# A two-layer mixture-of-experts block around a linear recurrence: value and gate projections formed during the inversion, silu by ScalarE alone, output projection ahead of the forget gate's products, roots by logarithm

## The reference, cut to what matters

```
x = x + 0.5 * ffn(layernorm(x))          # top 2 of 8 experts, x is [4, 1024, 256] float32
x = x + attn(layernorm(x))
x = x + 0.5 * ffn(layernorm(x))

attn:  q, k, v = silu(x@Wq), silu(x@Wk), silu(x@Wv)
       log_f = log_sigmoid(x @ Wf1 @ Wf2);  beta = 2*sigmoid(x @ Wbeta);  k = l2norm(k)
       recurrence over 1024 steps of a 32x32 state per head (decay, a rank-one correction, k v^T)
       y = out * sigmoid(x @ Wog1 @ Wog2);  y = y / sqrt(mean(y*y) + eps) * norm_w;  return y @ Wo
layernorm: (x - mean) / sqrt(var + eps)
```

## Time and profile before

| | |
|---|---|
| median of 3 runs (lowest, highest) | 2212.82 us (2205.81, 2214.22) |
| the profiled execution, its own time | 2211.96 us |
| its span, first to last instruction | 2210.2 us |
| mean granted TensorE clock | 0.846 of full speed |
| busy: PE, DVE, POOL, ACT | 1602.6 (73%), 1189.6 (54%), 735.4 (33%), 632.5 (29%) us |
| first layer of experts with its routing | 0 to 574 us |
| attention: begin; three looped passes; last pass | 574 to 638; 638 to 1490; 1494 to 1756 us |
| second layer of experts | 1758 to 2210 us |

### The profile page before, as it was taken

How to read it: one execution, slowest core, us unless ns; L and a number is a source line. 1 busy time by engine, 2 the same in 40 slices (tenths; PEclk the granted TensorE clock), 3 DMA queues, 4 the chain that set the end, 5 groups by cost and what they waited for, 6 DMA issues and landing times. The chain is left out here.

```text
span 2210.2 us, 62919 instructions
## 1 busy us (share of the span) xinstructions
PE 1602.6 (73%) x23284; PEld 1062.9 (48%) x23285; DVE 1189.6 (54%) x3478; ACT 632.5 (29%) x1646; POOL 735.4 (33%) x988
## 2 busy tenths in 40 slices
PE   4359999999477278572777536786357299999995
PEld 4336666666135265251643436444355156666663
DVE  7513434444256875559764696667766334344442
ACT  2111111111356234453343633446323111111110
POOL 3722222222044151550514704238044212222221
PEclk9999999999677587775887856886668599999998
DMA  9443223232101000110001000010000272323234
GB/s 293 146 160 48 45 45 45 46 45 39 52 3 28 1 19 20 41 30 0 20 20 40 10 20 15 5 58 9 3 11 29 95 233 45 48 43 48 43 48 100
DMA packets 83844, 113.32 MB, mean 51 GB/s; under 512 B 13048, under 2 KB 74944, under 8 KB 81600
## 3 DMA queue, kind: packets, MB, share of 16 engines
q1 hardware_dynamic: 57120, 75.91, 11.2%
q0 software_dynamic: 26592, 35.67, 9.7%
HBM read 63.65 MB, written 52.08 MB: 52 GB/s over the span
## 5 line engine op out<-in xcount | busy, mean ns | idle before, releaser
L591 PE MATMUL ffn_bank<-ffn_w,ffn_tileT 128*128 x1136 | 539.0, 597 | 7.4 <-DMA ffn_w<-in_w2t_dram 3.9
L712 POOL DMA_INDIRECT x<-ffn_yout,ffn_place x142 | 221.1, 1557 | 651.2 <-DVE ffn_yout L679 587.1
L650 ACT ACTIVATE ffn_gate<-ffn_bank 128x512 f32<-128x512 f32 x142 | 84.8, 597 | 706.2 <-PE ffn_bank L591 706.2
L607 PE MATMUL ffn_bank<-ffn_w,ffn_actT 128*128 x1136 | 268.6, 379 | 1.8 <-DVE ffn_actT L693 1.8
L591 PEld LDWEIGHTS ffn_bank<-ffn_w,ffn_tileT 128*128 128x128 f32 x1136 | 195.5, 192 | 148.7 <-issue 148.5
L607 PEld LDWEIGHTS ffn_bank<-ffn_w,ffn_actT 128*128 128x128 f32 x1136 | 215.7, 190 | 91.2 <-issue 69.2
L693 DVE COPY ffn_actT<-ffn_bank 128x512 f32<-128x512 f32 x142 | 98.1, 691 | 170.8 <-PE ffn_bank L599 170.8
L685 DVE TENSOR_TENSOR ffn_gate<-ffn_gate,ffn_bank 128x512 f32<-128x512 f32 x142 | 97.6, 687 | 167.1 <-PE ffn_bank L591 167.1
L1444 PE MATMUL at_bank<-pass_right,pass_left 32*32 32x48 f32 x3072 | 52.2, 231 | 83.0 <-DVE pass_right L1316 63.5
L580 PE MATMUL ffn_bank<-ffn_ident,ffn_tile 128*128 128x128 f32 x284 | 55.6, 278 | 77.5 <-DMA ffn_tile<-xs 77.3
L599 PEld LDWEIGHTS ffn_bank<-ffn_ident,ffn_gate 128*128 128x128 f32 x568 | 71.2, 141 | 73.9 <-issue 73.7
(11 more groups left out here) (493 smaller groups left out, 3252.1 us busy)
## 6 DMA issues: line engine op xcount, KB each, us to landing
ffn_tile<-xs SPq DMA_DIRECT2D x142, 130.0 KB, 2.1
ffn_w<-in_w1t_dram SPq DMA_DIRECT2D x16, 1024.0 KB, 5.2
ffn_w<-in_w2t_dram SPq DMA_DIRECT2D x16, 512.0 KB, 6.2
ffn_x<-in_x_dram SPq DMA_DIRECT2D x16, 256.0 KB, 4.8
x<-ffn_x SPq DMA_DIRECT2D x16, 256.0 KB, 6.1
pass_xa<-x SPq DMA_DIRECT2D x12, 256.0 KB, 3.6
pass_xr<-x SPq DMA_DIRECT2D x12, 256.0 KB, 2.7
x<-pass_xr SPq DMA_DIRECT2D x12, 256.0 KB, 2.1
```

Source lines behind the costliest of these rows:

```text
L591: t = pe.matmul(bank[:, :], rowsT[b][:, k * P:(k + 1) * P], w1[:, bass.ds(e * 2048 + (k * 1024 + half * INNER), INNER)], start=(k == 0), s ...
L607: t = pe.matmul(p_y[b], actT[b][:, k * P:(k + 1) * P], w2[:, bass.ds(e * 1024 + k * DIM, DIM)], start=(k == 0), stop=(k == ICH - 1))
L650: act.activation(gate[b][:, :], p_g[b][:, :], ACT.Silu).then_inc(s_silu, 1)
L712: pool.indirect_dma_start(total, bass.IndirectOffsetOnAxis(ap=place[b][:, 0:1], axis=0), yout[b][:, :], None, compute_op=ALU.add).then_inc ...
```

## The change

- Value and gate projections leave `between`. They are formed in `invert`, on TensorE between the groups n = 7 and n = 8 that go back, and on ScalarE ahead of the third `compact`. `xT` and `fg` therefore last: `fg` has a buffer of its own, `xT` lies in the buffer of the gate `gt`, so its first copy waits until o times gate is done.
- silu is one ScalarE activation; VectorE's second step, the halved weights and the tanh buffers go. The k and q jobs (8 instead of 16) use banks 0 to 2 and no longer wait for `log_f`. The sums of squares of k stand in banks 3, 2, 0, 1, so the products with beta no longer wait for their reading; the first of them waits for the slot numbers.
- In `between` the output projection stands ahead of `fg` and the forget gate's products on TensorE; `fg` is copied by ScalarE; `log_f` stands on VectorE inside `choose_vector`, ahead of the wait for the counts.
- 1/sqrt(var) is Exp(-0.5 Ln(var)) on ScalarE with one Newton step of three dependent VectorE instructions (`refine`) in place of Sqrt and a reciprocal, in all layer norms. The Ln/Exp set is loaded ahead of use.

```diff
+def refine(dve, link, root, var, tmp):
+    link(dve.tensor_tensor(tmp[:, :], root[:, :], root[:, :], ALU.mult))
+    link(dve.scalar_tensor_tensor(out=tmp[:, :], in0=tmp[:, :], scalar=-0.5, in1=var[:, :], op0=ALU.mult, op1=ALU.mult))
+    link(dve.scalar_tensor_tensor(out=root[:, :], in0=tmp[:, :], scalar=1.5, in1=root[:, :], op0=ALU.add, op1=ALU.mult))
...
-        r.link(dve, dve.reciprocal(r.rstd[:, :], r.rstd[:, :]))
+        refine(dve, lambda ins: r.link(dve, ins), r.rstd, r.var, r.dm)
...
-        act.activation(self.rstd[:, :], self.var[:, :], ACT.Sqrt).then_inc(self.s_std, 1)
+        act.activation(self.rstd[:, :], self.var[:, :], ACT.Ln).then_inc(self.s_ln, 1)
+        act.wait_ge(self.s_ln, g + 1)
+        act.activation(self.rstd[:, :], self.rstd[:, :], ACT.Exp, scale=-0.5).then_inc(self.s_std, 1)
...
+        fg = last("fg", [FG, BATCH * PT])
+        xT = gt[:, :, :].rearrange("p (k c) t -> p k (c t)", k=KCH)
...
-                for t in (wq, wk, wv):
-                    dve.tensor_scalar(t[:, :, :], t[:, :, :], 0.5, None, ALU.mult)
...
# between
+    JOBS = [(t, w, g, c) for t, w in ((k, wk), (q, wq)) for g, c in QUARTERS]
+    SQUARES = [psum[i] for i in (3, 2, 0, 1)]
-            r = routing(..., sem, [psum[i] for i in (0, 1, 2, 2, 3, 0)])
+            r = routing(..., sem, [psum[0], psum[1]] + [psum[3][:, i * P:(i + 1) * P] for i in range(4)])
# between, TensorE
+                    if j >= 3:
+                        pe.wait_ge(s_ev, j - 2)
+                    for kc in range(KCH):
+                        i = pe.matmul(psum[j % 3][:, :], w[:, kc, g * P:(g + 1) * P], xT[:, kc, c * 512:(c + 1) * 512], ...)
...
                 if ends:
                     pe.wait_ge(s_yn, 4)
                     (output projection, 8 tiles)
                 if begins:
+                    pe.wait_ge(s_xt, NT)
+                    (fg in two halves into psum[0], psum[1])
+                    pe.wait_ge(s_fgc, 2)
+                    (the forget gate's four products into psum[4 + j])
                 if ends:
                     r.gate_tensor(pe, 0)
                 if begins:
-                    for j in range(2, EARLY + 4):
+                    for j in range(4):
                         job(j)
                 if ends:
                     r.count_tensor(pe, 0)
                 if begins:
-                    for j in range(EARLY + 4, len(JOBS)):
+                    for j in range(4, 8):
                         job(j)
                     for j in range(4):
                         pe.wait_ge(s_sq, j + 1)
-                        pe.wait_ge(s_gt, j + 1)
+                        pe.wait_ge(s_ev, min(j + 5, 8))
+                        if j == 0 and ends:
+                            pe.wait_ge(r.s_rows, 1)
# between, ScalarE, after the copies to xT: the new order
+                    act.copy(fg[:, 0:512], psum[0][0:FG, :])
                     r.std_scalar(act, 0)
+                    act.copy(fg[:, 512:1024], psum[1][0:FG, :])
                     (Abs of the four forget products)
                     r.turn_scalar(act, 0)
                     (Exp of the four)
                     r.choose_scalar(act, 0)
                     (Ln of the four)
+                    act.preload_act_table_set("silu_and_others")
                     (silu of jobs 0 to 3; tanh of beta's rows; silu of jobs 4 to 7)
                     act.preload_act_table_set("natural_log_exp_and_others")
# between, VectorE
+                    r.logits_vector(dve, 0)
+                    r.choose_vector(dve, 0, (lambda: [log_f(j) for j in range(4)]) if begins else None)
# invert, TensorE
                 if n == 8:
+                    for j, (t, g, c) in enumerate(VALUES):
+                        if j < 4:
+                            pe.wait_ge(s_bke, j + 1)
+                            for kc in range(KCH):
+                                t = pe.matmul(psum[j][:, :], wv[:, kc, g * P:(g + 1) * P], xT[:, kc, c * 512:(c + 1) * 512], ...)
+                        else:
+                            pe.wait_ge(s_vale, j - 3)
+                            t = pe.matmul(psum[j % 4][:, :], wrank[RANK:2 * RANK, g * P:(g + 1) * P], fg[RANK:2 * RANK, c * 512:(c + 1) * 512], ...)
+                        t.then_inc(s_val, 1)
+                    pe.wait_ge(s_vale, len(VALUES))
                     pe.wait_ge(s_tc, 3)
# invert, ScalarE
                 if n == 8:
+                    act.preload_act_table_set("silu_and_others")
+                    for j, (t, g, c) in enumerate(VALUES):
+                        act.wait_ge(s_val, j + 1)
+                        (j < 4: Silu of psum[j] to v; else Tanh of psum[j % 4], scale 0.5, to gt)
                     act.wait_ge(s_inv, STEPS - LAST // 2 + CT)
                     compact(slice(CT, CT + CT // 2), slice(0, CT))
```

More of the change, by code:

```diff
@@ L126, in __init__ @@
         self.p_t, self.p_g, self.p_c = banks[0:2], banks[2:4], banks[4:6]
-        (self.s_stat, self.s_var, self.s_std, self.s_xn, self.s_tr, self.s_xt, self.s_gate, self.s_sub, self.s_exp,
+        (self.s_stat, self.s_var, self.s_ln, self.s_std, self.s_xn, self.s_tr, self.s_xt, self.s_gate, self.s_sub, self.s_exp,
          self.s_both, self.s_cnt, self.s_rows, self.s_own) = (
-            sem("r_" + n) for n in "stat var std xn tr xt gate sub exp both cnt rows own".split())
+            sem("r_" + n) for n in "stat var ln std xn tr xt gate sub exp both cnt rows own".split())
         k = 64
@@ L910, in between @@
         if ends:
-            r = routing(lambda n, sh, dt=F32: sb("r_" + n, sh, dt, at=scope), sem, [psum[i] for i in (0, 1, 2, 2, 3, 0)])
+            r = routing(lambda n, sh, dt=F32: sb("r_" + n, sh, dt, at=scope), sem, [psum[0], psum[1]] + [psum[3][:, i * P:(i + 1) * P] for i in range(4)])
             if not begins:
@@ L1054, in _ @@
                     if begins:
+                        if ends and j == 0:
+                            act.wait_ge(s_y, 4)
                         turn(2 * j)
@@ L1061, in _ @@
                 if begins:
-                    if not ends:
-                        act.preload_act_table_set("natural_log_exp_and_others")
+                    act.wait_ge(s_fg, 1)
+                    act.copy(fg[:, 0:512], psum[0][0:FG, :]).then_inc(s_fgc, 1)
+                if ends:
+                    r.std_scalar(act, 0)
+                if begins:
+                    act.wait_ge(s_fg, 2)
+                    act.copy(fg[:, 512:1024], psum[1][0:FG, :]).then_inc(s_fgc, 1)
                     for j in range(4):
@@ L1067, in _ @@
                         act.activation(lg[j][:, :], psum[4 + j][:, :], ACT.Abs).then_inc(s_a, 1)
+                if ends:
+                    r.turn_scalar(act, 0)
+                if begins:
                     for j in range(4):
@@ L1070, in _ @@
                         act.activation(lg[j][:, :], lg[j][:, :], ACT.Exp, scale=-1.0).then_inc(s_e, 1)
+                if ends:
+                    r.choose_scalar(act, 0)
+                if begins:
                     for j in range(4):
@@ L1171, in _ @@
                 if begins:
-                    for j in range(EARLY):
-                        silu(j)
-                if ends:
-                    r.logits_vector(dve, 0)
-                    r.choose_vector(dve, 0, (lambda: [silu(j) for j in range(EARLY, EARLY + 4)]) if begins else None)
-                if begins:
-                    for j in range(EARLY + 4 if ends else EARLY, NKQV):
-                        silu(j)
                     dve.wait_ge(s_bt, 1)
@@ L1495, in invert @@
 def invert(nc, scope, sb, sem, psum, s, env, a_sb, a_top, tk, s_tk, regroup, z, nxt):
-    ident, ta, mask = (env[n] for n in ("ident", "ta", "mask"))
+    ident, ta, mask, xT, fg, wv, wrank, v, gt = (env[n] for n in "ident ta mask xT fg wv wrank v gt".split())
     def tb(name, shape):
```

127 lines of the change are left out of this document (45 added, 82 removed).

## The result

| | before | after |
|---|---|---|
| median of 5 runs, us | 2212.82 (2205.81 to 2214.22) | 2195.89 (2193.78 to 2198.17) |
| profiled execution: span / own time, us | 2210.2 / 2211.96 | 2196.3 / 2198.17 |
| granted clock | 0.846 | 0.847 |

The ratio is 0.9929, interval 0.9905 to 0.9954: faster by 17 us, where I had forecast 36. 2195.9 lies above my range, which ended at 2194.

A forecast was written before the change was run, and what follows sets the result against it. Attention blocks were taken as bound by order and waits, looped passes ending with the scatter chain behind the slot numbers. Passes -17.6, `begin` -19.5, costs +1.6: -35.5 against 2211.96 gives 2176.5 us; range 2166 to 2194.

The forecast's parts named there:

- Value and gate in the inversion, cost 0: All four inversions: added projections fit ScalarE's 26.54 us idle before the third `compact`, ending over 5 us early; cost 0.
- Rival E: Inversion: the projections overflow it, by ScalarE's writes or a late start; 3 us x 4 = +12, 2188; chance 0.06.
- rival F: silu: Tanh not in its table set, two loads more in each place; `begin` 0 to 2.6 us; chance 0.05.
- `begin`, -19.5: `begin`: fewer jobs, fed without gaps, and a shorter k chain end it at 618.1 against 638.2; -19.5 taken.
- rival B: Clock stays low in jobs: each pass gives 2.7, `begin` 13; -19.5 in all, 2192; chance 0.20.
- (a) root, +0.4: Looped pass, layer norm root: three dependent 8-column instructions replace one, +0.4 us.
- (b) to (d): Looped pass: output projection first at 850.6 instead of 857.85, then `fg`, forget products, routing; softmax Exp to 876.1.
- (e), (f) slot numbers, -5.9 each: Looped pass: choice 6.8 us, counts to 886.1, scan to slot numbers 2.9; slot numbers at 889.0, 5.9 us earlier.
- Block end tied to the scatters: Looped passes: scatter chain, 22.4 us from slot numbers to landing, ends the block; only earlier slot numbers pay.
- Rivals C and D: C: scatters don't bind, 12 us a pass, 2158, chance 0.04. D: all `between` at 1.2 GHz, 2248, chance 0.04.
- Scan and decays unchanged: Scan and decays blocks: expected sign that their times stay as before the change; 0 in the sum.

The follow-up runs named there:

- E2: Kernel after with the value and gate projections back in `begin` and `between`, the inversion without them; 2191.81 us.
- E7: Kernel after with the products of `fg` and the forget gate ahead of the output projection again, on TensorE and in ScalarE's order; 2205.28 us.
- E5: Kernel after; in looped passes' `between`, key squares on VectorE and `log_f` both behind the slot numbers, counts behind the second k projection instead of the fourth; 2177.43 us.
- E8: Kernel before with 208 empty TensorE instructions at the end of `begin`, putting the decays' code where it stands in the kernel after; 2250.27 us.
- E1: Kernel after with 48 empty TensorE instructions (semaphore increments) added at the end of `begin`; 2189.11 us.
- E9: E5 with 112 empty TensorE instructions in a block ahead of `begin`; 2181.07 us.
- E10: E5 with 176 empty TensorE instructions in a block ahead of `begin`; 2201.32 us.

## Why the prediction was wrong

By its steps:

- **Value and gate in the inversion, cost 0**: right (E2: inversions 251.3 with, 250.7 without). The idle time ahead of the third `compact` shrank from 26.5 to 14.6 us, not to 7, because all jobs ran at 1.72 us. Rival E fell, and so did rival F: one table load at 715.35 serves the silu steps and the tanh steps behind it.
- **`begin`, -19.5**: right. 43.7 against 62.3 is -18.6. The 1.0 for the weights was to come ahead of it; from the attention's first load of x to `begin` it is 13.6 us instead of 14.1, so the profile shows 0.5. The first job stood at 596.2; the first instructions stood up to 0.86 us apart, at a granted clock of 0.57 up to 600.2, and the jobs behind them took 1.72 us each at 1.00: rival B fell there.
- **(a) root, +0.4**: too small. The third step of `refine` begins while GpSimd forms the second pair's squares and takes 1.04 us instead of 0.17, in all three passes.
- **(b) to (d)**: the order did what I said, and E7 prices it, clock and all, at 18.5 us of slot numbers in three passes. The softmax stood at 865.4, 41.4 us after the block's start; my 876.1 is 40.7 after it.
- **(e), (f) slot numbers, -5.9 each**: by the difference -3.4, -5.9 and -6.1, together -15.4 for -17.6. In absolute terms I said 53.6 us after the block's start and 56.1 came: 0.9 from the root and 2.3 from the three steps of the choice that lie beside GpSimd's squares, less the 0.7 by which I had taken the counts to be later than `log_f`. Passes 2 and 3 of before had been 2.5 us longer than the first, which hid this. The step that failed here is the 6.8 us of the choice, taken over from the earlier trace rows, where no GpSimd product ran beside it: it measured 9.1 (865.70 to 874.79).
- **Block end tied to the scatters**: right, to 0.1 us, and E5 shows that it holds further down. Rivals C and D fell.
- **"Scan and decays unchanged"**: this is the step that made the number wrong. None of its lines was edited, and I had put its cost at 0 without a further reason. Decays grew by 11.0 us: TensorE's stream ahead of them was 48 instructions shorter, and this shift alone costs 13.5 us with the code of before (E8) and 20.3 with that of after (E1). So something else in the change took up to 9.3 us off the decays (183.0 before, 173.7 in E1 at the same place); what that is no run shows. The last scan grew by 5.1 at clock 0.73 against 0.82; over the kernels here a scan took 71 us at 0.9 and 83 us at 0.56, with the same lines of code. What sets that clock was not settled. First and last experts scatter by up to 2 us between kernels that share their code (576.9 to 578.9, 476.5 to 478.9).

Sum: from my -35.5 to the profiled -13.9 are 21.6 us. Decays 11.0, last scan 5.1, slot numbers 2.2, first experts 2.3, last experts 2.0 and `end` 0.8 over forecast, less 1.8 by which inversions, other scans and the last decays were shorter: 21.6. The largest term could have been read from the kernel before: TensorE idle at "issue" inside groups of a straight-line block, at regular counts, and 12 products taken from ahead of it. I did not ask where those idle times would go.

## What to carry to other kernels

When instructions are moved out of or into a long unrolled program, look in every block behind them for idle time at regular counts of instructions: its place moves with them, and blocks that nobody edited change with it (here 57 to 66 us for one block). Time a change at two or three places of the code before judging it: by the stages, the move of the projections is worth 16 us, and the place at which it happened to put the decays costs 19. And when work goes to another engine's idle time, list what runs beside it: small VectorE steps beside a GpSimd product took four to six times their length.

## What the runs showed of the hardware

- Empty semaphore instructions on TensorE start 0.15 us apart (E8, E9, E10); 208 of them made `begin` 25.5 us longer (E8), 48 were free there (43.5 us in E1, 43.7 without), where TensorE was idle at the end.
- A 16 KB packet of TensorE's program is used up in 2.6 us by 32x32 products, and TensorE goes on 2.2 to 2.9 us behind the start of the next packet (380 of 381 cases in the decays; once 3.2), so it idled up to 2.8 us. Where it waits for VectorE in that time, no cut is seen.
- VectorE steps beside a GpSimd product of 1.04 us waited for its end when they were products of two SBUF tiles (L109, L232) or went from one SBUF tile to another (L226, L238). Steps with an input in PSUM did not: in the decays L1297 took 0.28 us beside GpSimd's products (630.80) as without them. The Trainium skill (GPSIMD Engine Reference, "8. Key points") says that the two engines share SBUF interfaces and that two-input and two-port VectorE instructions contend; here this was a full wait: L109 went from 0.17 to 1.04 us, to the end of the product.
- A table load took 1.28 us each time (30 before, 20 after). In 14 of the 20 loads after, the next activation followed within 0.01 us; the other six stand ahead of steps that wait for data.
